# Cross attention of a four-layer decoder: value products spread over a batch's tiles, and the square transpose in two instructions

## What is computed

```python
kv_rope = kv_c * cos + _rotate_half(kv_c) * sin
scores = jnp.einsum('bhsr,bhlr->bhsl', q_r, k_r)
attn = jax.nn.softmax(scores, axis=-1)
ctx_c = jnp.einsum('bhsl,bld->bhsd', attn, kv_rope)
```

## Time and profile before

| | |
|---|---|
| median of 3 runs | 3219.04 us (3218.99 to 3221.29) |
| the profiled execution, its own time | 3230.32 us |
| its span | 3228.3 us |
| PE busy | 2933.8 us, 91% of the span |
| DVE, ACT, POOL busy | 1862.5, 1242.3, 872.7 us |
| attention stage of layer 0, first to last turn on PE | 217.9 to 656.3 us |
| of layer 1 | 1343.6 to 1750.3 us |
| of layer 2 | 2303.5 to 2714.6 us |

### The profile page before, as it was taken

The page is one execution under the profiler, slowest core; times in us unless marked ns, Lnnn a source line. Parts: engine busy times, 40 slices in busy tenths (PEclk is TensorE's granted clock), DMA queues, the critical chain, the costliest instruction groups (busy, mean ns, idle before and its releaser), DMA issues. The chain is left out here.

```text
span 3228.3 us, 47818 instructions
## 1 busy us (share of the span) xinstructions
PE 2933.8 (91%) x17993; PEld 1709.2 (53%) x17997; DVE 1862.5 (58%) x3321; ACT 1242.3 (38%) x1997; POOL 872.7 (27%) x743
## 2 busy tenths in 40 slices
PE   4889998988999989899998989989899998677999
PEld 3655555554455453355555557753355555446444
DVE  6557887733232257788885233347788885655222
ACT  3446656521111142455554122222455653424221
POOL 4324555410316024433333000004333333201000
PEclk8899999988999989999999999999999999888999
DMA  1146677622122212277776010012277775001111
GB/s 32 48 120 161 166 174 166 145 66 95 63 91 78 88 28 81 62 165 158 158 165 162 13 42 25 25 43 74 65 170 155 166 168 125 15 12 23 39 39 33
DMA packets 221440, 299.21 MB, mean 93 GB/s; under 512 B 127178, under 2 KB 149052, under 8 KB 218764
## 3 DMA queue, kind: packets, MB, share of 16 engines
q1 hardware_dynamic: 220348, 294.39, 37.4%
q10 hardware_dynamic: 864, 1.77, 0.2%
HBM read 120.52 MB, written 21.38 MB: 44 GB/s over the span
## 5 line engine op out<-in xcount | busy, mean ns | idle before, releaser
L1786 ACT ACTIVATE l1x_shared<-l1x_shared,l1x_a_low 128x1500 f32<-128x1500 f32 x112 | 173.1, 1546 | 159.8 <-DVE l1x_shared L1740 156.9
L1786 ACT ACTIVATE l2x_shared<-l2x_shared,l2x_a_low 128x1500 f32<-128x1500 f32 x112 | 173.1, 1546 | 158.4 <-DVE l2x_shared L1740 156.8
L1786 ACT ACTIVATE l0x_shared<-l0x_shared,l0x_a_low 128x1500 f32<-128x1500 f32 x112 | 173.2, 1546 | 139.5 <-DVE l0x_shared L1740 138.1
L1656 PE MATMUL l0x_a_S_ps<-l0x_kt,l0x_a_q 64*128 64x366 f32 (+1 forms) x896 | 176.4, 507 | 4.4 <-issue 2.5
L1656 PE MATMUL l1x_a_S_ps<-l1x_kt,l1x_a_q 64*128 64x366 f32 (+1 forms) x896 | 175.9, 506 | 2.2 <-DVE l1x_shared L1740 1.9
L1656 PE MATMUL l2x_a_S_ps<-l2x_kt,l2x_a_q 64*128 64x366 f32 (+1 forms) x896 | 174.9, 505 | 2.0 <-DVE l2x_shared L1740 1.6
L2026 DVE TENSOR_TENSOR l0f_times_up<-l0f_gate,l0f_U 128x448 f32<-128x448 f32 x64 | 39.7, 621 | 236.9 <-PE l0f_U L1944 236.9
L1995 ACT ACTIVATE l0f_gate<-l0f_G 128x448 f32<-128x448 f32 x72 | 39.1, 543 | 310.7 <-PE l0f_G L1939 310.7
L1353 POOL TENSOR_TENSOR l2x_q_straight<-l2x_q_straight,l2x_q_crossed 128x448 f32<-128x448 f32 x48 | 54.5, 1135 | 340.5 <-DVE l2x_q_crossed L1344 340.5
L1740 DVE TENSOR_SCALAR_CACHE_REDUCE l0x_shared<-l0x_a_S_ps 128x768 f32<-128x768 f32 x112 | 107.3, 958 | 66.0 <-PE l0x_a_S_ps L1656 57.4
L1740 DVE TENSOR_SCALAR_CACHE_REDUCE l2x_shared<-l2x_a_S_ps 128x768 f32<-128x768 f32 x112 | 107.3, 958 | 53.7 <-PE l2x_a_S_ps L1656 50.2
(11 more groups left out here) (672 smaller groups left out, 6474.2 us busy)
## 6 DMA issues: line engine op xcount, KB each, us to landing
l0x_space<-normed SPq DMA_DIRECT2D x192, 128.0 KB
l1x_space<-normed SPq DMA_DIRECT2D x192, 128.0 KB
l2x_space<-normed SPq DMA_DIRECT2D x192, 128.0 KB
l0x_space<-l0x_a_blocks SPq DMA_DIRECT2D x186, 96.0 KB, 2.8
l1x_space<-l1x_a_blocks SPq DMA_DIRECT2D x186, 96.0 KB, 3.6
l2x_space<-l2x_a_blocks SPq DMA_DIRECT2D x186, 96.0 KB, 3.3
l0f_gu<-in_L_ffn_gu SPq DMA_DIRECT2D x36, 256.0 KB, 2.6
l0x_a_q<-l0x_qa SPq DMA_DIRECT2D x32, 224.0 KB, 4.0
```

Of the source, the lines that this page charges most:

```text
L1656: last = pe.matmul(S_ps[:, 2 * pair + rows_, 0:w], q[lane, b % 2, k * 128:(k + 1) * 128], kt[lane, b % 2, pair * W1:pair * W1 + w], start= ...
L1786: act.activation(p[:, n % 2], p[:, n % 2], ACT.Exp, bias=low[:, n % 2, 1:2], scale=-1.0, accum_out=den[:, b % 2, k:k + 1]).then_inc(exp_re ...
```

## The change

The diff moves slots of the value products between tiles; adds a piece, so that a group's last slots run a tile later than before; lets a tile run the end of one batch's group before the start of another's; shifts ScalarE's two context copies by one tile; and splits the square transpose into one of the six inner blocks and one of the two outer blocks, each with a semaphore of its own (pair 0 of `negate` overwrites the inner columns and pair 1 the outer ones).

```diff
-    PIECES = {5: (0, 0, 2), 6: (0, 2, 4), 7: (0, 4, 8), 8: (0, 8, 12), 9: (1, 0, 4), 10: (1, 4, 8), 11: (1, 8, 12)}
+    PIECES = {5: [(0, 0, 1)], 6: [(0, 1, 4)], 7: [(0, 4, 7)], 8: [(0, 7, 10)], 9: [(0, 10, 12), (1, 0, 1)],
+              10: [(1, 1, 5)], 11: [(1, 5, 9)], 12: [(1, 9, 12)]}
...
         def move(eng, b, g, lanes):
 
-            eng.wait_ge(blocked, T * b + FIRST[g] + COUNT[g])
+            eng.wait_ge(inner_blocked, T * b + FIRST[g] + COUNT[g])
+            eng.wait_ge(outer_blocked, T * b + FIRST[g] + COUNT[g])
...
                 def own(b, g):
 
-                    pool.wait_ge(blocked, T * b + FIRST[g] + COUNT[g])
+                    pool.wait_ge(inner_blocked, T * b + FIRST[g] + COUNT[g])
+                    pool.wait_ge(outer_blocked, T * b + FIRST[g] + COUNT[g])
...
-                    if k > 4:
-                        values(b, *PIECES[k])
-                    elif b > 0:
-                        values(b - 1, *PIECES[k + T])
+                    for piece in PIECES.get(k + T, []) if b > 0 else []:
+                        values(b - 1, *piece)
+                    for piece in PIECES.get(k, []):
+                        values(b, *piece)
                     if ctx is not None and k == 4 and b + 1 < B:
                         turn_keys(b + 1)
-                for k in range(T, T + 5):
-                    values(B - 1, *PIECES[k])
+                for k in range(T, T + 6):
+                    for piece in PIECES[k]:
+                        values(B - 1, *piece)
...
                         if pair == 0 and n > 1:
                             dve.wait_ge(turned, n - 1)
-                            dve.wait_ge(blocked, n - 1)
+                            dve.wait_ge(inner_blocked, n - 1)
                         if pair == 1:
                             dve.wait_ge(passed, 2 * n + 1)
+                            if n > 1:
+                                dve.wait_ge(outer_blocked, n - 1)
...
-                    dve.transpose(blocks[g][:, :, k - FIRST[g]].rearrange("q l j b -> q j l b"),
-                                  p[:, n % 2, 2 * KP:LK - 2 * KP].rearrange("q (j l b) -> q j l b", j=NB, l=4)).then_inc(blocked, 1)
+                    to = blocks[g][:, :, k - FIRST[g]].rearrange("q l j b -> q j l b")
+                    squares = p[:, n % 2, 2 * KP:LK - 2 * KP].rearrange("q (j l b) -> q j l b", j=NB, l=4)
+                    dve.transpose(to[:, 1:NB - 1], squares[:, 1:NB - 1]).then_inc(inner_blocked, 1)
+                    dve.transpose(to[:, 0:NB:NB - 1], squares[:, 0:NB:NB - 1]).then_inc(outer_blocked, 1)
...
-                    if k == 2 and b > 0:
+                    if k == 3 and b > 0:
                         keep_contexts(b - 1, 0)
-                    if k == 5 and b > 0:
+                    if k == 6 and b > 0:
                         keep_contexts(b - 1, 1)
```

More of the change, by code:

```diff
@@ L1469, in attend @@
         pt_kept = st.sem(name + "pt_kept")
-        blocked = st.sem(name + "blocked")
+        inner_blocked = st.sem(name + "inner_blocked")
+        outer_blocked = st.sem(name + "outer_blocked")
         moved = [[st.sem(f"{name}moved{g}{j}") for j in range(2)] for g in range(2)]
```

## The result

| | before | after |
|---|---|---|
| median | 3219.01 us (4 runs) | 3285.67 us (4 runs, 3278.05 to 3290.32) |
| ratio | | 1.0207, 95% interval 1.0183 to 1.0230 |
| span of the profiled execution | 3228.3 | 3281.1 |
| first to last tile's turn, layer 0 | 437.9 | 503.4 |
| the same, layer 1 | 406.2 | 404.4 |

The kernel became 66.7 us slower; 3278 was forecast, with 3257 to 3294 as the range. The two profiled executions lie 52.8 us apart, and only there can the loss be placed: layer 0 is 65.5 us longer, layers 1 and 2, which run the same changed loop, are 1.8 and 11.8 shorter.

What follows compares the result with a forecast made beforehand. PE was taken as the limit; 59 us of layer 0 waits, plus 8 for its clock, minus 8 gained in layers 1 and 2, plus 0 for the split, gave 3219 + 59 = 3278 us, range 3257 to 3294.

Steps and rivals of the forecast that it cites:

- PE's work is the same and its tiles even: All layers: the same slots spread over tiles of 3.42 to 3.65 us, seven summing to 24.7 before and after.
- The chain valued, rope, own, group 0's inner slots: Layer 0: rope starts 9.29 us after tile 4 begins, so PE waits 3.83 us for POOL's copies in 13 batches.
- DVE's lag behind it, 0.87 a batch: Layer 0, after PE's wait for POOL's copies: DVE is late too, so PE waits 0.87 us more a batch.
- The clock, 8 us: Layer 0: PE's clock falls behind three of four of the 13 waits, costing 0.8 us each, 8 in all.
- The forecast's upper bound, 22: Layer 0: the most that PE's clock falls could cost, 13 x 1.7 = 22 us.
- rival A: PE's clock falls every time and for longer, 22 us or more, no gain in layers 1 and 2: 3300; 10%.
- The sum for layer 0: Layer 0: 59 us of waits plus 8 for PE's clock; its stretch about 65 us longer.
- the small lags of tiles 0 and 1: Layer 0, kernel before: small waits of PE behind DVE, about 0.3 us seven times, 2 us taken off the loss.
- the SyncE step: Layer 0: store_values waits for rope, so move(b, 1) behind it starts 3.3 us later, at no cost.
- Layers 1 and 2, 8 gained: Layers 1 and 2: PE's waits for group 1's moved squares up to 0.99 us shorter each; 8 us gained of 12.
- The split, nothing: Square transpose in two on DVE: added instruction at most 0.157 us, pair 0 saves a 0.15 wait; taken as zero.

Runs made afterwards that it cites:

- 1: Changed kernel with a fourth buffer of values in layer 0 and the rotation in place: 0.9920 of the kernel before.
- 2: Changed kernel, but in layer 0 group 1's last three slots run at the end of tile 4, ahead of turn_keys: 0.9964 of the kernel before.
- 3: Kernel before, with only rope in layer 0 waiting in addition for the turn of tile 6: 1.0273 of the kernel before.
- 5: Changed kernel with 9 extra unread matmuls on PE in layer 0, tile 0, ahead of its wait for group 0's carried squares: 3268.2 us, 1.0120 of the kernel before.
- 4: Changed kernel with 16 extra unread matmuls on PE in layer 0, tile 0, ahead of its wait for group 0's carried squares: 1.0176 of the kernel before.
- 6: The changed kernel itself, run again unaltered: 3287.2 us, 1.0177 of the kernel before.
- 8: Changed kernel with the square transpose in one instruction again, so the spread of slots alone: 1.0152 of the kernel before.
- 9: Kernel before with the spread order and a fourth buffer of values in layer 0, square transpose in one instruction: 0.9954 of the kernel before.
- 10: Kernel before with only a fourth buffer of values in layer 0 added: 0.9994 of the kernel before.
- 7: Kernel before with only the square transpose split in two instructions: 0.9961 of the kernel before.

## Why the prediction was right, step by step

*PE's work is the same and its tiles even*: right. In layers 1 and 2 an undisturbed batch takes 24.76 both times, and after the change its tiles take 3.43 to 3.65, where they took 3.10 to 3.97.

*The chain valued, rope, own, group 0's inner slots*: right in place, count and nearly in size, and shown by taking it away in two ways (1, 2) and by making it alone (3). rope at 9.39 for 9.29; a wait of 4.15 for 3.83, as rope to the end of the copies took 9.96 for 9.85 and PE resumed 0.15 behind them.

*DVE's lag behind it, 0.87 a batch*: sized wrongly. I read 3.54 from a transpose to the scores' pair 1, in the old kernel. With the split it is 441.97 - 438.66 = 3.31 (5), and 3.31 - 2.67 leaves 0.64. Tiles 0 and 1 of 5 say the same: 11.87 - 7.07 - 4.15 = 0.65. In the changed kernel itself this lag lies under the low clock.

*The clock, 8 us*: the term that was most mis-sized. Two things: it fell 13 times in 13 and not in three of four, and at seven of the 13 it stayed low 6.8 us and not 3.4, where the earlier trace rows had shown me a fall of the short kind. Tiles 0 and 1 together take 13.41 for 7.07 of work: 6.34 a batch. Less the wait that is 2.2 a batch for DVE's lag and clock, where I had 0.87 + 0.6. Held up by work, the clock gave back 20 us (5). The forecast's upper bound, 22, was near the right value. The earlier trace rows are windows of 4 us, too short to tell the two kinds of fall apart: of the six falls that I had counted in the kernel before two were of the long kind (at 562.7 and 2678.9), as its trace shows. What counts is the part of a fall that lies behind the wait: 58.6 us in the 13 batches, half of which is 2.25 a batch, as much as the 2.2 found. Without the low clock 0.65 of it comes back as DVE's lag. The rule of the Trainium skill (TensorE: Matmul & The Clock Gate, "HAM oscillation — how this bites in real kernels"), that waits repeated in a loop bring the half clock each time, held here in all 13, and I should have given it more than rival A's 10%.

*The sum for layer 0* then came out right by cancellation, which is luck. Forecast were 59 + 8 = 67, and the stage is 503.4 - 437.9 = 65.5 longer. But the chain cost 13 x 6.34 = 82. Against it stands what the old profile held and the new one doesn't: the small lags of tiles 0 and 1, 3.4 us, where I took off 2; waits for moved squares of group 1 in layer 0, 7.5 us, with what followed them 9.7; and 3 us in the first batch, 24.1 for 27.3. With PE held for rope the squares of group 1 had landed when they were needed: in the six traces with that wait, or with work in its place (the change, 3, 4, 5, 6, 8), layer 0 has no such wait for landed squares between its turns, in the six others it has 1 to 4. I had claimed the SyncE step at nothing (right) and not counted the old waits as saved. Over the whole program the profiled executions, 3230.3 and 3283.7, lie 53 apart for 59 forecast, the medians 67; no trace places the other 13.

*Layers 1 and 2, 8 gained*: the profiles say 1.8 and 11.8, but 6 us of the latter are within the scatter, since layer 2 takes 398.9 in one trace of the changed kernel and 404.9 in the other (6). The waits for landed squares went from nine to six and from 23.8 to 15.0 us. The runs say 0.45% for the order over the whole kernel (9 beside 10), some 14 us with 7 to 23 as the interval of 9. Traces don't place it: the waits for landed squares between the turns sum to 35.0 us in 9 and 49.1 in 10, but to 31.3 in the kernel before. Why landings are late at some batches and not at others I didn't test.

*The split, nothing*: it gave 0.21 us a round of DVE and 0.4% (7). Still, the added instruction isn't free: where the next one waits for nothing, the two take 0.06 us more than the one (1.22 for 1.16). The 58 cycles an instruction of the Trainium skill (VectorE: DVE Perf Modes, "The TRN2 errata"), 0.06 us at 0.96 GHz, agree with it. The round is shorter all the same, since the next instruction no longer waits for the whole transpose: with that wait the one took 1.39 from start to start, without it 1.16.

## What to carry to other kernels

A step that is moved "one tile later" is later by everything that stands between, here a turn of keys and its wait that only one of three layers has: 5.6 us for a tile of 3.5. Look up each semaphore that the moved instruction raises, and find the waiter with the least slack; it may be an engine that seems idle, with 0.75 us to spare. And where a loop gains a wait of some microseconds on PE each round, count the low clock at every one of them: here it cost 1.5 us a round by itself beside a wait of 4.15, and with DVE's lag 2.2.

## What the runs showed that I had not expected

- Two short transposes (768 and 256 elements) take 0.90 and 0.32 us from start to start, together 0.06 more than one of 1024 that nothing waits for (1.16), and 0.17 less than one whose end the next instruction waits for (1.39).
- Fp32 matmuls of 64 columns of weights that write the two halves of the partitions in turn run two at a time: a pair of records of 256 columns starts every 0.216 us, and one record every 0.216 when all write the same half (experiment 4).
- Waits of 4.15 us on PE, alike from batch to batch, brought low clock of 3.4 us in six batches and of 6.8 in seven, and in ten of the 13 it began before PE went on.
